# Attention queries held as three bf16 parts, and the one-hot product over them in three bf16 passes

## The reference, cut to what matters

```
q, k, v = h @ wq + bq, h @ wk + bk, h @ wv + bv
scores  = sum(q[dst] * k[src]) * D**-0.5 + (edge_weight * we + be)
exp_s   = exp(scores - segment_max(scores, dst)[dst])
out     = segment_sum(v[src] * exp_s / denom[dst], dst)
```

## Time and profile before

| what | us |
|---|---|
| median of three executions | 5067.49 |
| span of the profiled execution (first to last instruction) | 6606.6 |
| busy: PE / DVE / ACT / POOL | 3748.5 / 3700.6 / 1475.8 / 3595.2 |
| mean granted TensorE clock | 0.868 |

### The profile page before, as it was taken

One profiled execution on the slowest core, in us unless ns is written; L12 is line 12 of the kernel. 1 busy time (PEld: TensorE's weight loads), 2 busy tenths in 40 slices (PEclk: granted clock), 3 DMA queues, 4 the chain that ended last, 5 costly groups with the idle time before them and its releaser, 6 DMA issues. The chain is left out here.

```text
span 6606.6 us, 98591 instructions
## 1 busy us (share of the span) xinstructions
PE 3748.5 (57%) x15612; PEld 2748.4 (42%) x15613; DVE 3700.6 (56%) x12722; ACT 1475.8 (22%) x5078; POOL 3595.2 (54%) x4000
## 2 busy tenths in 40 slices
PE   0000020005776776776677777777779667777676
PEld 0000010004555554555455555555559534444443
DVE  5249691006666666666555555555557656555555
ACT  1000000000111111111455455555546301100000
POOL 4640686755655565555444444444437766655554
PEclk9999999998887888888788888878889878888888
DMA  4320224454444444444333333333332233333332
GB/s 119 85 68 0 73 83 89 118 148 120 127 127 123 125 128 124 127 128 111 93 94 94 96 95 95 94 93 94 97 95 86 89 88 94 91 91 90 90 90 72
DMA packets 505174, 651.54 MB, mean 99 GB/s; under 512 B 86113, under 2 KB 381294, under 8 KB 504944
## 3 DMA queue, kind: packets, MB, share of 16 engines
q0 software_dynamic: 150160, 395.04, 20.9%
q1 hardware_dynamic: 354913, 255.45, 14.3%
HBM read 550.09 MB, written 100.06 MB: 98 GB/s over the span
## 5 line engine op out<-in xcount | busy, mean ns | idle before, releaser
L1398 POOL DMA_INDIRECT a_row<-h_rows,a_idx x832 | 789.8, 949 | 944.0 <-PE a_p_s L1504 396.0
L2005 POOL DMA_INDIRECT r_row<-h_rows,r_idx x832 | 798.3, 960 | 528.7 <-PE r_p_s L2046 267.9
L462 POOL DMA_INDIRECT src_records<-rec,pos_slot x784 | 808.2, 1031 | 419.6 <-issue 250.3
L983 POOL DMA_INDIRECT s_row<-h_rows,s_rec x832 | 804.5, 967 | 281.0 <-issue 242.2
L1018 PE MATMUL s_sums<-s_row,s_hotw 128*128 128x256 f32 x1664 | 661.3, 484 | 519.5 <-DVE s_hotw L1203 315.3
L2046 PE MATMUL r_p_s<-r_row,r_hot 128*128 128x272 f32 x1664 | 644.8, 502 | 362.8 <-DVE r_row L2182 171.9
L1481 PE MATMUL a_p_q<-nodes,a_hotT 128*128 x1664 | 665.0, 486 | 314.9 <-DVE a_score L1551 188.9
L1211 DVE TENSOR_TENSOR nodes<-nodes,s_sums 128x385 f32 x832 | 455.5, 548 | 509.1 <-remote 290.8
L1504 PE MATMUL a_p_s<-a_row,a_masked 128*128 128x257 f32 x1664 | 588.7, 439 | 178.1 <-issue 124.3
L2046 PEld LDWEIGHTS r_p_s<-r_row,r_hot 128*128 128x128 f32 x1664 | 353.1, 234 | 678.8 <-issue 296.2
L1551 DVE CUSTOM_DVE_ANT_0 a_prod<-a_p_q,a_row 128x258 f32<-128x258 f32 x832 | 352.7, 424 | 415.9 <-DMA s_rec<-src_records 187.6
(11 more groups left out here) (315 smaller groups left out, 7511.6 us busy)
## 6 DMA issues: line engine op xcount, KB each, us to landing
s_rec<-src_records SPq DMA_DIRECT2D x832, 66.0 KB
a_locs<-dloc_rows SPq DMA_DIRECT2D x208, 256.0 KB
rec<-in_edge_attr SPq DMA_DIRECT2D x98, 448.0 KB
s_row<-h_rows,s_rec POOLq DMA_INDIRECT x832
a_row<-h_rows,a_idx POOLq DMA_INDIRECT x832
r_row<-h_rows,r_idx POOLq DMA_INDIRECT x832
src_records<-rec,pos_slot POOLq DMA_INDIRECT x784
x_rows<-X SPq DMA_DIRECT2D x1, 6272.0 KB
```

What stands on the lines that cost most here:

```text
L462: gp.indirect_dma_start(out=src_records, out_offset=bass.IndirectOffsetOnAxis(ap=pos_slot[:, k:k + 1], axis=0), in_=rec[:, k, :], in_offse ...
L983: gp.indirect_dma_start(out=row[:, k % R, :], out_offset=None, in_=env["h0_rows"], in_offset=bass.IndirectOffsetOnAxis(ap=rec[:, k % R, DS ...
L1398: gp.indirect_dma_start(out=row[:, k, 0:D], out_offset=None, in_=env["h2_rows"], in_offset=bass.IndirectOffsetOnAxis(ap=idx[:, k:k + 1], a ...
L2005: gp.indirect_dma_start(out=row[:, k % R, 0:D], out_offset=None, in_=env["h3_rows"], in_offset=bass.IndirectOffsetOnAxis(ap=idx[:, k:k + 1 ...
```

## The change: three bf16 parts

Queries are stored as high, middle and low part: high is the query rounded to bf16, middle the rounded rest, low what is left. Their sum is the float32. Each block's row in `nodes` grows from 385 to 387 words, which hold three pieces of 258 bf16 columns (257 of the query, and one for the edge weight's term: 1 in the first piece, 0 in the others). `make_q` on VectorE now writes a float32 tile, ScalarE copies it to the high part, VectorE subtracts, ScalarE copies the middle part, VectorE subtracts again and writes the low part. In `ask` one float32 product becomes three bf16 products that accumulate in the same PSUM bank. Their one-hot matrix is the upper half of each float32 word of `hotT`, read with a step of two.

```diff
-            env["nodes"] = sb(mid, "nodes", [P, BLOCKS, NW])
+            env["nodes"] = sb(mid, "nodes", [P, BLOCKS, NODE_W])
...
+    HIGH, REST, MIDDLE, LOW = 49, 50, 51, 52
...
+                def high_part(q, k, first):
+                    b = ranked(q, ACT_E)
+                    ac.wait_ge(S["q_ready"], q + 1)
+                    nc.scalar.activation(at(split, b)[:, 0:D + 1], asked[:], ACT.Copy).then_inc(S["q_high"], 1)
+
+                def middle_part(q, k, first):
+                    b = ranked(q, ACT_E)
+                    ac.wait_ge(S["q_rest"], q + 1)
+                    nc.scalar.activation(at(split, b)[:, QW:QW + D + 1], rest[:], ACT.Copy).then_inc(S["q_middle"], 1)
...
                 def make_q(q, k, first):
-                    b = ranked(q, DVE_E)
                     ve.wait_ge(S["h2_qk"], q + 1)
...
-                    nc.vector.tensor_tensor(at(acc, b)[:, 0:D + 1], p_q, qkb[:], ALU.add).then_inc(S["q_ready"], 1)
+                    nc.vector.tensor_tensor(asked[:], p_q, qkb[:], ALU.add).then_inc(S["q_ready"], 1)
+
+                def rest_of_q(q, k, first):
+                    b = ranked(q, DVE_E)
+                    ve.wait_ge(S["q_high"], q + 1)
...
+                    nc.vector.tensor_tensor(rest[:], asked[:], at(split, b)[:, 0:D + 1], ALU.subtract).then_inc(S["q_rest"], 1)
+
+                def low_part(q, k, first):
+                    b = ranked(q, DVE_E)
+                    ve.wait_ge(S["q_middle"], q + 1)
+                    v = at(split, b)
+                    nc.vector.tensor_tensor(v[:, 2 * QW:2 * QW + D + 1], rest[:], v[:, QW:QW + D + 1], ALU.subtract
+                                            ).then_inc(S["q_low"], 1)
...
-                    nc.tensor.matmul(p_q[k % 2], hotT[:, k % F, :], query[:, bass.ds(b, 1), 0:RW].rearrange("p a d -> p (a d)"),
-                                     start=True, stop=True).then_inc(S["asked"], 1)
+                    hot = hotT[:, k % F, :].bitcast(BF16).rearrange("p (n w) -> p n w", w=2)[:, :, 1]
+                    for part in range(PARTS):
+                        rows = query[:, bass.ds(b, 1), part * QW:(part + 1) * QW].rearrange("p a d -> p (a d)")
+                        last = nc.tensor.matmul(p_q[k % 2], hot, rows, start=part == 0, stop=part == PARTS - 1)
+                    last.then_inc(S["asked"], 1)
```

More of the change, by code:

```diff
@@ L49 @@
 NW = D + ED + 1
+PARTS = 3
+QW = D + 2
+NODE_W = QW * PARTS // 2
 META = 4
@@ L814, in sources_and_layers_0_1 @@
     nc, A, c, sb, ps, sem = (env[k] for k in ("nc", "A", "c", "sb", "ps", "sem"))
-    acc = env["nodes"]
+    nodes = env["nodes"]
+    acc = nodes[:, :, 0:NW]
+    split = nodes[:].bitcast(BF16)
     R, H = SLOT, UNROLL
@@ L864, in sources_and_layers_0_1 @@
         turned_h = sb(ctx, "turned_h", [P, DC, P])
+        asked, rest = sb(ctx, "n_asked", [P, D + 1]), sb(ctx, "n_rest", [P, D + 1])
         half = sb(ctx, "n_half", [P, 1])
@@ L881, in sources_and_layers_0_1 @@
                  "z_added", "gate_added1", "terms_ready", "h1_ready", "h1_added", "x2_ready", "h2_ready", "h2_turned",
-                 "h2_copied", "h2_qk", "q_ready", "z_in")
+                 "h2_copied", "h2_qk", "q_ready", "q_high", "q_rest", "q_middle", "q_low", "z_in")
         S = {n: sem("n_" + n) for n in names}
@@ L1165, in copy_h2 @@
                     nc.scalar.activation(turned_h[:], p_t[:, 0:DC, :], ACT.Copy).then_inc(S["h2_copied"], 1)
+                def high_part(q, k, first):
[6 more added lines that the diff above has]
+                    nc.scalar.activation(at(split, b)[:, QW:QW + D + 1], rest[:], ACT.Copy).then_inc(S["q_middle"], 1)
                 once = {17 + 4 * n: [copy_weights(n)] for n in range(2 * DC)}
                 once[17 + 8 * DC] = [copy_product]
-                woven(ac, once=once, nodes=[(COPY_H, copy_h2), (NORM2, norm_x2), (NORM1, norm_x1), (SIG, gates), (COPY, copy_turned),
+                woven(ac, once=once, nodes=[(DVE_LEAD + MIDDLE, middle_part), (DVE_LEAD + HIGH, high_part), (COPY_H, copy_h2), (NORM2, norm_x2), (NORM1, norm_x1), (SIG, gates), (COPY, copy_turned),
                                             (STAGE, stage)])
@@ L1299, in make_q @@
                         ve.wait_ge(S["w_copied"], 2 * DC + 3)
-                    ve.wait_ge(S["staged"], q + 1)
-                    nc.vector.tensor_tensor(at(acc, b)[:, 0:D + 1], p_q, qkb[:], ALU.add).then_inc(S["q_ready"], 1)
+                    else:
+                        ve.wait_ge(S["q_rest"], q)
+                    nc.vector.tensor_tensor(asked[:], p_q, qkb[:], ALU.add).then_inc(S["q_ready"], 1)
+                def rest_of_q(q, k, first):
+                    b = ranked(q, DVE_E)
+                    ve.wait_ge(S["q_high"], q + 1)
+                    if not first:
+                        ve.wait_ge(S["q_low"], q)
+                    nc.vector.tensor_tensor(rest[:], asked[:], at(split, b)[:, 0:D + 1], ALU.subtract).then_inc(S["q_rest"], 1)
[5 more added lines that the diff above has]
+                                            ).then_inc(S["q_low"], 1)
                 woven(ve, (LAG, add), (1, weigh), (0, hots), once={24: [key_bias]}, begin=load_blocks,
                       nodes=[(DVE_LEAD + p, s) for p, s in (
-                          (QUERY, make_q), (SHIFT2, shift(1)), (EPS2, add_eps(1)), (AVG2, average(1)), (STAT2, statistics(1, "x2_ready")),
+                          (LOW, low_part), (REST, rest_of_q), (QUERY, make_q), (SHIFT2, shift(1)), (EPS2, add_eps(1)), (AVG2, average(1)), (STAT2, statistics(1, "x2_ready")),
                           (X2, make_x2), (H1, add_h1), (SHIFT1, shift(0)), (G2, add_gate(1, "gate_added1", "terms_ready")),
@@ L1315, in attention @@
     nc, A, c, sb, ps, sem = (env[k] for k in ("nc", "A", "c", "sb", "ps", "sem"))
-    query, acc = env["nodes"], env["sums"]
+    acc = env["sums"]
+    query = env["nodes"][:].bitcast(BF16)
     R = 4 * UNROLL
@@ L1504, in sum_rows @@
                     nc.tensor.matmul(p_s[k % 2], masked[:, k % F, :], row[:, k, 0:D + 1], start=True, stop=True).then_inc(S["summed"], 1)
-                pe.wait_ge(S["begun"], 6)
+                pe.wait_ge(S["begun"], 8)
                 in_turns(pe, TILES, R, (ASK, ask), (SUM, sum_rows), (MASK_T, turn_masked), (LOOK, look_up),
@@ L1514, in _ @@
                     ve.nop().then_inc(filled, 1)
-                nc.vector.memset(query[:, :, D + 1:D + 2], 1.0).then_inc(S["begun"], 1)
+                for part in range(PARTS):
+                    column = part * QW + D + 1
+                    nc.vector.memset(query[:, :, column:column + 1], 0.0 if part else 1.0).then_inc(S["begun"], 1)
                 nc.vector.memset(acc[:], 0.0).then_inc(S["begun"], 1)
@@ L1521, in _ @@
                                         ).then_inc(S["begun"], 1)
-                ve.wait_ge(S["begun"], 4)
+                ve.wait_ge(S["begun"], 6)
                 nc.vector.tensor_scalar(reset[:], reset[:], RESET, None, ALU.mult).then_inc(S["begun"], 1)
                 nc.vector.memset(m[:, 0:Q], LOWEST).then_inc(S["begun"], 1)
-                ve.wait_ge(S["begun"], 6)
+                ve.wait_ge(S["begun"], 8)
                 blocks = []
```

## The result

The changed kernel takes 5169.2 us (median of 4 runs, 5166.0 to 5173.1), the one before 5069.8 on the same chip. The ratio is 1.0199 with a 95% interval of 1.0185 to 1.0214: 2% slower, 100 us, where 25 us less were forecast.

A forecast was written before the change was run, and what follows sets the result against it. GpSimd was taken as the main bound: 4324 us in a row plus 523 between walks, 4847 of 5067. Attention -35 and the split +10 gave -25, so 5042 us; own range 5000 to 5055, 8-in-10 range 4965 to 5110.

The forecast's parts named there:

- `ask` on TensorE: Attention: three bf16 passes take 0.36 us where one float32 product took 0.52, saving 0.16 us per tile.
- The case of dear passes: Rival, attention: a bf16 pass costs as much as a float32 record, 0.215 us; +108, 5175 us; chance 6%.
- With TensorE 0.2 us under the others, I let 35 of the 50 us go: Attention: a faster TensorE removes 35 of some 50 us that GpSimd idles there; bounds 0 and -110.
- The rival without room: Rival: GpSimd's 1.25 us per tile sets attention already and the split hides; 5067 us; chance 19%.
- I take +10 us for all of this: Second stage: the split's added subtractions, copies and waits cost 10 us in all; bounds +2 and +56.
- the hand-over case: Rival, second stage: the hand-over between VectorE and ScalarE holds up the stage, +50; 5105 us; chance 16%.
- the cover: Second stage: VectorE's 22.3 us per block hides behind GpSimd's 25.5; without that, the split costs 56 us.
- The tail between the stages: After the second stage's last block: the chain of copies and subtractions is longer once, by some 2.5 us.
- The case on the slower side: Rival, second stage: VectorE and ScalarE wait on each other, +50, attention gives back 10; 5105 us; chance 16%.

The follow-up runs named there:

- e8: Changed kernel with 9 fillers fewer in prepare and none ahead of attention, second stage's and attention's loops in 3 blocks: 5098.7 us, ratio 1.0063.
- e14: The code of e8 with one bf16 pass in attention in place of three: 5097.6 us, ratio 1.0061.
- e4: Changed kernel with 20 fillers fewer in prepare and 30 fewer ahead of attention's loop: 5083.8 us, ratio 1.0035.
- e5: Kernel before plus the split's two copies and two subtractions alone, float32 product kept, fillers cut to 126 in prepare and 3 ahead of attention: 5081.5 us, ratio 1.0029.
- e3: Kernel before plus the split's two copies and two subtractions per block alone, queries and attention float32: 5197.4 us, ratio 1.0262.
- e7: Kernel before with 24 fillers more ahead of attention's loop and 24 fewer ahead of the relations': 5071.9 us, ratio 1.0008.
- e10: Kernel before with 52 fillers more ahead of attention's loop and 26 fewer ahead of the relations': 5194.5 us, ratio 1.0257.
- e11: Kernel before with 36 fillers more in prepare and 36 fewer ahead of attention: 5064.8 us, ratio 0.9996.
- e9: The code of e8 measured once more, as the intended edit had not been made: 5094.3 us.

## Why the prediction was wrong, step by step

- **`ask` on TensorE: right.** 0.34 us (0.36 forecast, bounds 0.32 and 0.65), a round of 1.02 (1.04). The case of dear passes is excluded.
- **"With TensorE 0.2 us under the others, I let 35 of the 50 us go": wrong in mechanism and size.** It gives nothing (attention in e8, e14 and before: 1066.8, 1066.7, 1067.7 us). In the second recording of before the two hardly wait for each other (within attention, to be held against the earlier trace rows, which have 148.6 and 188.9 us):

```profile
DVE a_prod L1551 <- PE a_p_q L1481: 6.0, 7, 2.7
PE a_p_q L1481 <- DVE a_score L1551: 0.3, 1, 0.3
```

  Attention was 1068 us, not 1090, against 1040 for GpSimd alone. Of the 28 us left, 10 are one wait for `a_idx` at the start of the stage, and most of the rest are waits of half a microsecond, one or two a turn. The rival without room (19%) was the right account of this step.
- **"I take +10 us for all of this": mis-sized, inside its bounds of +2 and +56.** With the fetching taken out and the passes worth nothing, the split costs 32 us (e8). The instructions last about what was said, and the copies less (419 ns to make the query, 423 and 427 for the subtractions, 421 and 420 for the copies), and none waits long: 1.4 and 3.3 us in 49 blocks, so the hand-over case (16%) was not it either. What was missed is that the subtractions lengthen instructions of GpSimd, the very engine called the cover; the trace shows this for `n_rstd`, and for the gathers the cause is open. The tail between the stages was priced at 2.5 us and is 6 to 10 (47.9 us after, 37.6 to 42.0 in the runs of before).
- **The step that failed was not in the list.** The sum had a term for what each added instruction does where it runs and none for where it puts the instructions behind it. 55 more instructions ahead of attention's loop moved it from 3 blocks to 4, for 92 us. The `FILLERS` and `range(38)` of empty operations on VectorE stood in the code, and the prediction did not ask what they were for. The packets of queue 14 stood on the page, 73 in all: with none in the loops of the walks, there was something to lose.
- **The other direction was priced by the wrong mechanism.** The case on the slower side gave 5105 us for a hand-over (its own terms, +50 and -10, make 5107); the time was 5169, outside the range of 4965 to 5110. With attention's loop in 3 blocks the changed kernel takes 5084 to 5099 us, which that range holds; the forecast of 5042 was wrong for that kernel too.

As a sum from the trace's walks: attention +92 (its place), second stage +7 and the tail +10 (the split, which costs less in the fetched loops of after, e4 and e5 than in e8, though not in e3), the rest -4; together 106 us in the recordings and 100 in the medians.

## What to carry to other kernels

Before adding instructions to an engine whose loops are long, count where each loop of that engine will lie: an edit in one stage cost 9% of another stage here that it doesn't touch, and 50 empty operations taken out put it right. Look for instruction packets inside loops in the DMA view, and for an idle time by "issue" that returns once a turn. A product made cheaper on an engine that is not last gave nothing, and work hidden "behind" GpSimd is only hidden if GpSimd's own instructions stay as short as they were.

## What the hardware showed that was not expected

The page "Advanced Engine Details and Errata" of the Trainium skill, section "ISA Cache", gives 32 KB in two lines of 16 KB, 256 instructions each. The traces show packets of 8 KB, and a loop of 315 instructions (20 KB) that touches four of them is fetched already; the measurement decides here.
- The same loop of 315 instructions is not fetched at 2512 to 2826 (e7) and is fetched at 2540 to 2854 (e10); the positions between were not tried.
- The same fetching costs attention 92 to 129 us. In the kernel before it costs the second stage nothing that can be measured (e11), where VectorE has 100 us of waiting for it to hide in.
- TensorE with less to do was granted less clock, a mean over its levels of 1.2 and 2.4 GHz (0.5 and 1): 1.00 in attention before, 0.96 with three bf16 passes, 0.94 with one; it is the same in the other runs (1.00 in e5 without the passes, 0.96 in e4 and e9 with three, and 0.95 in e10, where before's own code stops once a turn). Its float32 `sum_rows` products took 380 ns before, 405 with three passes, 424 with one. Part of what the passes save is lost in that way; no row had shown it, and the prediction priced nothing for it.
